# Wide self-attention on one core: probabilities turned by VectorE and DRAM instead of TensorE, softmax shift and bias copy on GpSimd

## The reference, cut to what matters

```python
x = x + _L0_attn_ref(_layernorm(x, axis=-1), L0_attn_Wq, L0_attn_Wkv, L0_attn_Wout, L0_attn_bout, L0_attn_rel_emb)

def _L0_attn_ref(x, Wq, Wkv, Wout, bout, rel_emb):
    q = (x @ Wq).reshape(B, N, h, dh).transpose(0, 2, 1, 3) * scale
    kv = x @ Wkv
    k, v = (kv[..., :dh], kv[..., dh:])
    sim = jnp.einsum('bhid,bjd->bhij', q, k)
    bias = rel_emb[rp_bucket]
    sim = sim + bias.transpose(2, 0, 1)[None] * bias_scale
    sim = jnp.where(causal[None, None], -jnp.finfo(sim.dtype).max, sim)
    attn = jax.nn.softmax(sim, axis=-1)
    out = jnp.einsum('bhij,bjd->bhid', attn, v)
    out = out.transpose(0, 2, 1, 3).reshape(B, N, h * dh)
    return out @ Wout + bout
```

## Time and profile before

| | |
|---|---|
| median of 3 runs | 2317.92 us (2317.68 to 2318.93) |
| profiled execution | 2314.49 us, span 2312.7 us |
| TensorE busy (matmul / weight load) | 2059.0 us (89%) / 1736.3 us (75%) |
| VectorE busy | 1834.0 us (79%) |
| ScalarE busy | 1599.4 us (69%) |
| GpSimd busy | 1220.3 us (53%) |
| DMA data moved | 96.96 MB |

### The profile page before, as it was taken

One profiled execution on the slowest core, in us unless ns is written; L12 is line 12 of the kernel. 1 busy time (PEld: TensorE's weight loads), 2 busy tenths in 40 slices (PEclk: granted clock), 3 DMA queues, 4 the chain that ended last, 5 costly groups with the idle time before them and its releaser, 6 DMA issues. The chain is left out here.

```text
span 2312.7 us, 89168 instructions
## 1 busy us (share of the span) xinstructions
PE 2059.0 (89%) x32143; PEld 1736.3 (75%) x32143; DVE 1834.0 (79%) x5229; ACT 1599.4 (69%) x4229; POOL 1220.3 (53%) x1280
## 2 busy tenths in 40 slices
PE   7999999997888862439999979999899999999997
PEld 6898898885666641227888858888688888888886
DVE  4888888876899976987777667777588888888885
ACT  1766677666888876537888858888566666666664
POOL 1333333336899963009999869999233333333332
PEclk9999999998999996758999979999999999999998
DMA  5000000001111100010000000000133333333333
GB/s 130 3 0 0 0 0 0 0 1 29 34 34 35 35 18 1 1 37 2 0 0 0 0 2 1 0 0 0 35 122 116 121 118 117 116 119 122 118 115 94
DMA packets 112238, 96.96 MB, mean 42 GB/s; under 512 B 24259, under 2 KB 103430, under 8 KB 112134
## 3 DMA queue, kind: packets, MB, share of 16 engines
q1 hardware_dynamic: 108722, 94.39, 13.5%
q10 hardware_dynamic: 3412, 1.19, 0.3%
HBM read 53.59 MB, written 41.94 MB: 41 GB/s over the span
## 5 line engine op out<-in xcount | busy, mean ns | idle before, releaser
L711 POOL TENSOR_TENSOR sa_sc<-sa_sc,sa_rs 128x1024 f32<-128x1024 f32 x64 | 122.0, 1906 | 309.0 <-DVE sa_rs L687 309.0
L1883 POOL TENSOR_TENSOR lo_qk_r<-lo_qk_ms,w_neg_half 128x20 f32<-128x20 f32 x64 | 227.0, 3547 | 22.4 <-DVE lo_qk_ms L1805 22.4
L1883 POOL TENSOR_TENSOR gl_qk_r<-gl_qk_ms,w_neg_half 128x20 f32<-128x20 f32 x64 | 226.5, 3539 | 14.4 <-DVE gl_qk_ms L1805 14.1
L487 POOL TENSOR_TENSOR xan_ve<-xan_mv,w_eps_ln 128x1 f32<-128x1 f32 x64 | 12.3, 192 | 388.8 <-DVE xan_mv L481 388.8
L921 ACT ACTIVATE xa_vx<-xa_oo 64x512 f32<-64x512 f32 x256 | 151.4, 592 | 20.2 <-PE xa_oo L822 13.9
L653 ACT ACTIVATE sa_oT<-sa_oo 128x512 f32<-128x512 f32 x128 | 69.5, 595 | 117.0 <-PE sa_oo L596 117.0
L934 ACT ACTIVATE xa_oT<-xa_oo 128x512 f32<-128x512 f32 x128 | 69.5, 594 | 115.5 <-PE xa_oo L870 115.5
L832 PEld LDWEIGHTS xa_qs<-xan_xT,late_x_wq 128*128 128x128 f32 x1024 | 124.4, 192 | 30.6 <-issue 30.6
L1026 POOL TENSOR_TENSOR xa_sc<-xa_sc,xa_rs 128x1024 f32<-128x1024 f32 x64 | 122.0, 1906 | 32.8 <-DVE xa_rs L986 32.8
L560 PE MATMUL sa_qs<-san_xT,w_a_wq 128*128 128x128 f32 x1024 | 132.4, 283 | 5.0 <-DVE sa_sc L673 3.6
L881 PE MATMUL xa_yy<-late_x_wo,xa_oT 128*128 128x128 f32 x1024 | 128.4, 280 | 1.7 <-ACT xa_oT L934 1.7
(11 more groups left out here) (326 smaller groups left out, 6563.1 us busy)
## 6 DMA issues: line engine op xcount, KB each, us to landing
blocks<-xa_tb SPq DMA_DIRECT2D x64, 512.0 KB, 2.6
xa_pt<-blocks SPq DMA_DIRECT2D x256, 128.0 KB, 2.9
w_x<-in_x_dram SPq DMA_DIRECT2D x8, 512.0 KB, 7.3
ca_cx<-in_ctx_dram SPq DMA_DIRECT2D x64, 64.0 KB, 1.8
ctxT_kept<-ca_xcT SPq DMA_DIRECT2D x64, 64.0 KB, 1.6
xa_cT<-ctxT_kept SPq DMA_DIRECT2D x64, 64.0 KB, 2.5
out_dram<-xa_out SPq DMA_DIRECT2D x64, 64.0 KB, 2.0
ca_mask<-in_mask_BxSxS_ff_dram SPq DMA_DIRECT2D x64, 32.0 KB, 1.7
```

The costliest lines, as they stand in the source:

```text
L711: pool.tensor_tensor(v, v, bcast(rs[:, s, :], 2, S), ALU.mult).then_inc(prob_done, 1)
L1883: pool.tensor_tensor(qk_r[:, s, :], qk_ms[:, s, :], k["neg_half"][:, 0:NQK], ALU.pow).then_inc(sg["qk_r"], 1)
```

## The change

In the wide self-attention, TensorE no longer turns the probabilities, and ScalarE no longer copies them. VectorE turns them in 32x32 blocks (`turn_blocks`), SyncE writes them to DRAM and reads them back spread (`spread_blocks`), through the same two DRAM buffers that the last stage uses later. The tile `sa_pt` has the layout of the last stage's, so the attention product writes its PSUM banks in another order and `outT` reads them so. The subtraction of the maximum and the copy of X plus bias move to GpSimd, the normalised input to ScalarE (with an offset that GpSimd makes in two more instructions). VectorE does the residual behind the maximum. `sc` has four buffers instead of two, `vx` eight instead of four. The lists have new lags, and the loop body is eight steps instead of four on all engines but SyncE, where it is two.

The diff, cut to its core:

```diff
+            @block.sync
+            def _(sp):
+                def spread_blocks(t, s):
+                    after(sp, blocks_done, t)
+                    sp.dma_start(k["blocks"][s][:, :], tb[:, s, :, :, :].rearrange("p q n i -> p (q n i)")).then_inc(parked[s], 16)
+                    landed(sp, parked, t, s)
+                    for q in range(4):
+                        sp.dma_start(pt[q * 32:q * 32 + 32, s, :, :, :, :].rearrange("p a e m i -> p a (e m i)"),
+                                     k["blocks"][s].rearrange("(a p) (q n) -> q p a n", a=4, q=4)[q]).then_inc(spread[s], 16)
+
+                skewed(sp, NT, [(5, spread_blocks)])
...
-                def turn_probs(t, four):
...
-                    after(pe, p_done, t, per=2)
+                    blocks_spread(pe, t, s)
...
-                                last = pe.matmul(oo[u][e * 64:e * 64 + 64, :].rearrange("p (m b i) -> p m b i", m=4, b=2)[:, :, b, :],
-                                                 vx[r, four, (b + u) % 2, :], pt[r, s, e, :, b, :], start=True, stop=True)
+                                last = pe.matmul(oo[u][e * 64:e * 64 + 64, b * 256:(b + 1) * 256], vx[r, four, (b + u) % 2, :],
+                                                 pt[r, s, 2 * b:2 * b + 2, e, :, :], start=True, stop=True)
...
-                skewed(pe, NT, [(2, scores), (4, attend), (1, key_value), (1, queries), (3, turn_probs), (4, output), (0, turn)], 4)
+                skewed(pe, NT, [(3, scores), (7, attend), (2, key_value), (2, queries), (7, output), (1, turn)], 8)
...
-                def probsT(t, four):
...
+                def apply(t, four):
+                    s = four % 2
+                    after(act, off_done, t)
+                    after(act, norm["xT_psum"], t, 2)
+                    act.activation(norm["xn"][:, s, :], tile_of(X, t), ACT.Identity, bias=off[:, s:s + 1],
+                                   scale=norm["rstd"][:, s:s + 1]).then_inc(norm["xn_done"], 1)
...
-                skewed(act, NT, [(4, outT), (1, key_value), (1, queries), (2, exponent), (3, probsT), (0, turned)], 4)
+                skewed(act, NT, [(1, apply), (7, outT), (2, key_value), (2, queries), (3, exponent), (1, turned)], 8)
...
-                    after(dve, p_psum, t, 2, per=2)
+                    after(dve, blocks_done, t, 4)
...
-                    dve.tensor_reduce(mx[:, s, :], v, AX.X, ALU.max).then_inc(max_done, 1)
-                    after(dve, max_done, t)
-                    dve.tensor_tensor(v, v, bcast(mx[:, s, :], 2, S), ALU.subtract).then_inc(shifted, 1)
+                    after(dve, shifted, t, 2)
+                    dve.tensor_reduce(mx[:, s, :], sc[:, four % 4, :, :, :].rearrange("p e c j -> p (e c) j"), AX.X, ALU.max).then_inc(max_done, 1)
+
+                def turn_blocks(t, four):
+                    s = four % 2
+                    after(dve, prob_done, t)
+                    blocks_spread(dve, t, s, 2)
+                    after(dve, o_psum, t, 2)
+                    dve.transpose(tb[:, s, :, :, :],
+                                  sc[:, four % 4, :, :, :].rearrange("p e (m u) (h j) -> p (u h) (e m) j", u=2, h=2)).then_inc(blocks_done, 1)
...
-                skewed(dve, NT, [(5, residual), (0, measure), (2, softmax), (0, apply), (4, copy_x), (2, sums)], 4)
+                skewed(dve, NT, [(3, softmax), (8, residual), (5, turn_blocks), (0, measure), (4, sums)], 8)
...
+                    pool.tensor_tensor(neg_mean[:, s:s + 1], norm["mv"][:, s, 0:1], neg_one[:, :], ALU.mult).then_inc(nm_done, 1)
+                    norm_rsqrt(k, norm, pool, t, s)
+                    after(pool, norm["rstd_done"], t)
+                    pool.tensor_tensor(off[:, s:s + 1], neg_mean[:, s:s + 1], norm["rstd"][:, s:s + 1], ALU.mult).then_inc(off_done, 1)
+
+                def shift(t, four):
+                    s = four % 2
+                    after(pool, max_done, t)
+                    v = sc[:, four % 4, :, :, :].rearrange("p e c j -> p (e c) j")
+                    pool.tensor_tensor(v, v, bcast(mx[:, s, :], 2, S), ALU.subtract).then_inc(shifted, 1)
...
-                skewed(pool, NT, [(0, rsqrt), (2, normalise)], 4)
+                def copy_x(t, four):
+                    after(pool, x_done, t, 2)
+                    pool.tensor_tensor(xb[:, four % 2, :], tile_of(X, t), k["a_row"][:, :], ALU.add).then_inc(xb_done, 1)
...
+                skewed(pool, NT, [(3, shift), (0, rsqrt), (4, normalise), (6, copy_x)], 8)
```

More of the change, by code:

```diff
@@ L533, in wide_self_attention, with blocks_spread @@
         exp_done, sum_done, inv_done, prob_done = sem("exp"), sem("row_sum"), sem("inverse"), sem("probs")
-        p_psum, p_done, o_psum, o_done = sem("probsT_psum"), sem("probsT"), sem("outT_psum"), sem("outT")
+        blocks_done, o_psum, o_done = sem("blocks_turned"), sem("outT_psum"), sem("outT")
+        parked = [sem(f"blocks_parked{s}") for s in range(2)]
+        spread = [sem(f"blocks_spread{s}") for s in range(2)]
+        off_done, nm_done, minus = sem("offset"), sem("neg_mean"), sem("minus_one")
+        def blocks_spread(eng, t, s, back=0):
+            if isinstance(t, int) and t - back < 0:
+                return
+            eng.wait_ge(spread[s], (t - s - back) * 32 + 64)
         y_psum, xb_done, x_done = sem("y_psum"), sem("x_plus_bias"), sem("x")
         with nc.Block() as block:
+            @block.sync
[8 more added lines that the diff above has]
+                skewed(sp, NT, [(5, spread_blocks)])
             @block.tensor
@@ L622, in key_value @@
                     act.activation(kT[:, s, :], misc[:, P:2 * P], ACT.Copy).then_inc(k_done, 1)
-                    after(act, o_psum, t, 4)
+                    after(act, o_psum, t, 8)
                     act.activation(vx[:, four, 0, :], misc[:, 2 * P:2 * P + DH], ACT.Copy).then_inc(v_done, 1)
@@ L638, in exponent @@
                     after(act, shifted, t)
-                    act.activation(sc[:, s, :, :, :], sc[:, s, :, :, :], ACT.Exp).then_inc(exp_done, 1)
-                def probsT(t, four):
+                    act.activation(sc[:, four % 4, :, :, :], sc[:, four % 4, :, :, :], ACT.Exp).then_inc(exp_done, 1)
+                def apply(t, four):
                     s = four % 2
[L643 to L646, removed]
+                    after(act, off_done, t)
+                    after(act, norm["xT_psum"], t, 2)
+                    act.activation(norm["xn"][:, s, :], tile_of(X, t), ACT.Identity, bias=off[:, s:s + 1],
+                                   scale=norm["rstd"][:, s:s + 1]).then_inc(norm["xn_done"], 1)
                 def outT(t, four):
@@ L693, in residual @@
                     dve.tensor_tensor(tile_of(X, t), yy[:, 0:D], xb[:, s, :], ALU.add).then_inc(x_done, 1)
-                def copy_x(t, four):
-                    s = four % 2
-                    after(dve, x_done, t, 2)
-                    dve.tensor_tensor(xb[:, s, :], tile_of(X, t), k["a_row"][:, :], ALU.add).then_inc(xb_done, 1)
-                skewed(dve, NT, [(5, residual), (0, measure), (2, softmax), (0, apply), (4, copy_x), (2, sums)], 4)
+                skewed(dve, NT, [(3, softmax), (8, residual), (5, turn_blocks), (0, measure), (4, sums)], 8)
             @block.gpsimd
@@ L704, in rsqrt @@
                 def rsqrt(t, four):
-                    norm_rsqrt(k, norm, pool, t, four % 2)
+                    s = four % 2
+                    after(pool, norm["mv_done"], t)
+                    pool.tensor_tensor(neg_mean[:, s:s + 1], norm["mv"][:, s, 0:1], neg_one[:, :], ALU.mult).then_inc(nm_done, 1)
[7 more added lines that the diff above has]
+                    pool.tensor_tensor(v, v, bcast(mx[:, s, :], 2, S), ALU.subtract).then_inc(shifted, 1)
                 def normalise(t, four):
```

23 lines of the change are left out of this document (12 added, 11 removed).

## The result

| | before | after |
|---|---|---|
| median of 4 runs | 2317.80 us | **2301.05 us** (2297.70 to 2303.86) |
| ratio to before | | 0.9929, 95% interval 0.9910 to 0.9947 |
| profiled execution | 2314.49 us, span 2312.7 | 2303.86 us, span 2302.0 |

Faster by 0.7%, as forecast in sign, but 30 us over the predicted 2271 and 5 us over the end of its range. In the profile the stage ends at 513.64 + 0.29 = 513.9 us instead of 528.2: 14.3 us less, of which this execution gave 3.6 back in stages that the change doesn't touch (its span is 10.7 us shorter).

What follows compares the result with a forecast made beforehand. TensorE alone was taken to bound the wide self-attention; 0.87 us less per step, after jumps, late transfers, fill and drain, ends the stage at 481.9 instead of 528.2: 2317.9 - 46 = 2271 us, range 2260 to 2296.

Steps and rivals of the forecast that it cites:

- Five jumps back at 0.48: 2.4: Wide self-attention loop of eight tiles per pass: five jumps back cost 0.48 us each, 2.4 us in all.
- Rival A: TensorE's longer loop no longer stays loaded; five jumps back cost 8 to 25 us, time 2280 to 2296; chance 0.19.
- The chances: Forecast range 2260 to 2280 got 0.60, A 0.19, B 0.09, C 0.06, D 0.06; faster 0.88, same 0.03, slower 0.09.
- The step: Plain step of the wide self-attention loop: without TensorE's turns, 7.32 - 0.87 = 6.45 us, bound by TensorE.
- Transfers: Blocks through DRAM arrive 1.4 us before the attention product needs them; late writes cost 3 us, bounds 0 and 30.
- Rival B: Block transfers set the beat, DMA engines near 55% used, attention product waiting in most steps; 2290 to 2305; chance 0.09.
- Rival C: VectorE's block turn cannot run beside GpSimd's shift, so the step is 7.6 us; time 2339; chance 0.06.
- the forecast's sum for VectorE: VectorE per step: 6.21 - 1.85 + 1.24 = 5.60 us, with waits on its own results 5.9 of 6.45.
- Fill and drain: Stage's ends: first scores at 43.4 us, four filling steps 25 us, drain 27.5 us against 19 before.

Runs made afterwards that it cites:

- the aligned kernel: The changed kernel with TensorE's loop in the wide self-attention starting at a multiple of 256 instructions; 2279.09 us (ratio 0.9839).
- the kernel of four tiles: The changed kernel with TensorE's and ScalarE's loops at four tiles per pass, values two steps later, four buffers of values and turned input; 2262.61 us (0.9765).

## Why the prediction was wrong

- **What failed: the price of the jump back.** The sum had "Five jumps back at 0.48: 2.4"; they cost 37.9 us. Rival A named this mechanism, its place and its sign (a pause at each eighth step with instruction fetches in the loop), and priced it at 1.7 us times one to three, 8 to 25 us in all. The 1.7 came from the entry of the last stage's loop: a loop entered for the first time, not a jump back, and at a piece's boundary (its list ends in `whole_blocks=True`). In the trace of before TensorE stands in that step for no more than 0.55 and 0.77 us:

```profile
1750.42 1.16 PE L857 MATMUL xa_qs<-xa_kT,xa_qT 64*64 64x64 f32 x64 [0.55 <-issue]
...
1753.27 0.33 PE L870 MATMUL xa_oo<-xa_pt,xa_vx 64*64 64x64 f32 x4 [0.77 <-issue]
```

A jump back to a piece that isn't loaded costs more even with one wait: 3.2 us over a plain step in the aligned kernel, 2.3 in the old one with eight tiles. The changed loop's start lies 11 matmuls before a boundary, so each jump pays two waits of 2.4 to 3.0 us, and the lower clock afterwards adds 1.65 to 2.9. Neither was in the price: a jump cost 7.6 us on average, more than the three times 1.7 that rival A allowed, and the time ended 5 us over A's own 2280 to 2296. The Trainium skill (Runtime: NRT & Kernel Launch, Instruction fetch mechanics) says that fetching ahead goes straight on and that a taken jump to a place outside the two pages held at the time stalls for a fetch. Runs with and without a loop agree on the first and on the stall, and put 1.8 to 3.2 us on the target's wait; they don't agree on two pages, since TensorE's body of 3.8 pieces jumps back without a fetch.
- **The chances failed with it.** The text counted 1880 instructions against a longest proven loop of 1480 and still put 0.19 on the case. The Trainium skill (Advanced Engine Details and Errata, ISA Cache) gives TensorE 128 KB in lines of 16 KB, which makes eight, an estimate from the page's figures; by that an early start in a piece would have been enough. The aligned kernel shows that it isn't: seven stay, eight are fetched again.
- **The step: right.** 7.32 - 0.87 = 6.45 forecast, 6.45 measured, with TensorE busy throughout. VectorE: 258.28 / 300 x 6.45 = 5.55 us of work per step in the kernel of four tiles (5.60 forecast, 5.9 with its own waits); GpSimd 244.86 / 300 x 6.45 = 5.26 (5.68).
- **Transfers: right in kind.** A margin of 1.4 us and 3 us of late writes were forecast. In the changed kernel's loop five writes take 4.2 to 4.8 us to the reads behind them where 2.75 is usual, one at each jump; TensorE doesn't wait for them: the step with the jump is itself some 7 us longer. Without a loop late writes cost 4.8 us, in the aligned kernel 2.7 before the first jump. Rival B did not come: in the kernel of four tiles the DMA engines are half busy and the step is 6.45.
- **Rival C did not come**: turn and shift run side by side at their lengths. By the forecast's sum for VectorE, 5.9 of 6.45, the shift's 1.23 doesn't fit there and the copy's 0.28 does; the runs agree, with 41 us for the one and at most 4 for the other.
- **Fill and drain: near.** These are the stage's ends in the changed kernel, TensorE's first and last scores and VectorE's last residual:

```profile
43.22 0.99 PE L594 MATMUL sa_qs<-sa_kT,sa_qT 64*64 64x64 f32 x53 [0.67 <-ACT sa_qT L645]
...
484.91 1.16 PE L594 MATMUL sa_qs<-sa_kT,sa_qT 64*64 64x64 f32 x64
...
513.64 0.29 DVE L708 TENSOR_TENSOR w_x<-sa_yy,sa_xb 128x128 f32<-128x128 f32 x1 [3.99 <-PE sa_yy L616]
```

First scores 43.2 (43.4 forecast), four filling steps to 66.5 or 23.3 us (25), drain 513.9 - 484.9 = 29.0 (27.5). With 35.5 for the jumps, -3.0 for late transfers that TensorE did not wait for, -1.7 for the fill, -0.2 for the first scores, -0.1 for rounding and +1.5 for the drain, the stage ends 32.0 us behind the forecast 481.9: the 513.9 of the trace. Nothing is left over. That the kernel without a loop comes to 2271.5 us, the very forecast, is partly luck: it has no jumps (2.4 less than the sum) and a shorter fill, against 4.8 us of late writes and a drain of 29.9.

## What to carry to other kernels

Unrolling has a price when the body outgrows what the engine keeps loaded: count the instructions of a loop, matmuls with their loads and waits, and look for the instruction queue among the DMA queues of its stretch. If it fetches, shorten the body (here by giving the values a later step, so that four buffers of them are enough and a pass needs only four tiles), or write the loop out; starting it at a piece's boundary gives back only part. And when a price is taken from a similar event elsewhere, look at the waits inside that event first. Here it was the first entry into an aligned loop, whose two waits summed to 1.3 us, and it stood for a jump back, which has waits of another size.

## What the runs showed of the hardware

- A loop of TensorE that touches seven pieces of 256 instructions (some 1710 in all) is kept; one that touches eight (some 1950) is fetched anew in every pass, nine pieces each time.
- A jump back to a piece that isn't loaded waits 1.8 to 3.2 us, and another 1.7 to 2.7 where the next boundary is near (11 or 31 matmuls behind the target); straight code of 64 tiles shows no such wait.
- After the two waits of a jump the granted clock was 0.50 to 0.53 for 3.3 us; in five jumps the lower clock cost 11.2 us on top of 26.7 us of standing.
- 192 increments of a semaphore in TensorE's queue took about 28 us, 0.15 each.
- A block turn of 128x1024 on VectorE and a tensor-tensor of the same size on GpSimd, started together, take 1.23 and 1.90 us, no longer than apart.
